# Four value-table buffers in the first stage, and another order of work at the opening of the second attention

## The reference

```python
def gat(x, adj, weight, linear_i, linear_j):           # layer 0, 8 heads of 64
    wh = (x @ weight).reshape(n, 8, 64)
    awh_i = (wh * linear_i).sum(axis=2); awh_j = (wh * linear_j).sum(axis=2)
    e = leaky_relu(awh_i[:, None, :] + awh_j[None, :, :], 0.2)
    e = e + ((1.0 - adj) * -1e10)[:, :, None]
    a = softmax(e, axis=1)
    return einsum('ijh,jhf->ihf', a, wh).reshape(n, 512)

def attention(x, adj, Wks, Wqs, Wvs, Wo):              # layer 1, 8 heads of 64
    adj = maximum(adj, eye)
    q, k, v = (einsum('nd,hdk->hnk', x, W) for W in (Wqs, Wks, Wvs))
    scores = einsum('hqk,hmk->hqm', q, k) * 64 ** -0.5
    scores = scores + 0.01 * eye - 1e16 * (1.0 - adj)
    return einsum('hqm,hmk,hko->qo', softmax(scores, axis=-1), v, Wo)

x = layernorm(x + gat(x, adj, ...))
x = layernorm(x + attention(x, adj, ...))
```

## Time and profile before

| | us |
|---|---|
| median of 3 runs | 4261.97 (4261.85 to 4263.58) |
| the profiled execution's own time | 4264.08 |
| its span, first to last instruction | 4260.6 |
| TensorE clock granted over the span | 0.952 of full |

### The profile page before, as it was taken

How to read it: one execution, slowest core, us unless ns; L and a number is a source line. 1 busy time by engine, 2 the same in 40 slices (tenths; PEclk the granted TensorE clock), 3 DMA queues, 4 the chain that set the end, 5 groups by cost and what they waited for, 6 DMA issues and landing times. The chain is left out here.

```text
span 4260.6 us, 104547 instructions
## 1 busy us (share of the span) xinstructions
PE 3773.0 (89%) x42884; PEld 2512.9 (59%) x42884; DVE 3499.7 (82%) x6039; ACT 3344.7 (79%) x4233; POOL 439.5 (10%) x635
## 2 busy tenths in 40 slices
PE   7981399999999969919999999999999999999977
PEld 4540399999999924405555555555555555555533
DVE  6655699999999977638888888888888888888734
ACT  3433699999999822209999999999999999999932
POOL 1211100000000000020120201201112011120000
PEclk9995699999999979959999999999999999999989
DMA  9988855555554377662453534444445354353133
GB/s 347 392 287 210 242 175 170 184 188 189 189 188 164 121 206 238 209 174 71 116 138 90 142 95 119 133 101 131 107 108 138 93 142 109 95 143 93 45 111 138
DMA packets 364121, 674.35 MB, mean 158 GB/s; under 512 B 79584, under 2 KB 239408, under 8 KB 326784
## 3 DMA queue, kind: packets, MB, share of 16 engines
q1 hardware_dynamic: 296448, 574.83, 45.3%
q0 software_dynamic: 24064, 84.37, 6.5%
q10 hardware_dynamic: 43136, 8.53, 1.0%
HBM read 524.43 MB, written 143.20 MB: 157 GB/s over the span
## 5 line engine op out<-in xcount | busy, mean ns | idle before, releaser
L1230 DVE CUSTOM_DVE_ANT_0 m_junk<-m_rough,m_rows 128x1024 bf16<-128x1024 f32 x1024 | 1253.5, 1224 | 287.8 <-PE m_rough L1097 226.3
L1179 ACT ACTIVATE m_scores<-m_strip 128x1024 f32<-128x1024 fp8e4 x1024 | 1052.3, 1028 | 102.4 <-POOL m_strip L1028 37.9
L1193 ACT ACTIVATE m_whole<-m_scores 128x1024 int32<-128x1024 f32 x1024 | 1038.0, 1014 | 35.9 <-PE m_scores L1130 25.5
L630 PE MATMUL g_acc<-g_vals,g_pos 128*128 128x130 f16 x8192 | 956.4, 218 | 48.6 <-DVE g_neg L585 48.6
L547 ACT ACTIVATE g_step<-g_arow,k_steep 128x512 fp8e4<-128x512 f32 x1536 | 948.6, 707 | 40.2 <-DVE g_pos L578 37.2
L630 PE MATMUL g_acc<-g_vals,g_neg 128*128 128x130 f16 x8192 | 955.8, 221 | 0.0
L1111 PE MATMUL m_acc<-m_v,m_halves 128*128 128x129 f16 (+1 forms) x16384 | 897.1, 208 | 45.2 <-ACT m_got L1156 45.2
L1111 PEld LDWEIGHTS m_acc<-m_v,m_halves 128*128 128x128 f16 x16384 | 751.0, 98 | 279.8 <-issue 186.5
L630 PEld LDWEIGHTS g_acc<-g_vals,g_pos 128*128 128x128 fp8e4 x8192 | 801.9, 98 | 59.5 <-DVE g_neg L585 37.1
L1125 PE MATMUL m_scores<-m_qA,m_kA 128*128 128x512 f16 x2048 | 780.7, 381 | 5.7 <-ACT m_scores L1179 5.6
L630 PEld LDWEIGHTS g_acc<-g_vals,g_neg 128*128 128x128 fp8e4 x8192 | 784.9, 96 | 0.0
(11 more groups left out here) (161 smaller groups left out, 3005.2 us busy)
## 6 DMA issues: line engine op xcount, KB each, us to landing
g_vals<-scr_gat_v SPq DMA_DIRECT2D x128, 1040.0 KB, 5.1
m_v<-scr_v SPq DMA_DIRECT2D x64, 1032.0 KB, 7.9
a_stage<-in_adj SPq DMA_DIRECT2D x64, 1024.0 KB, 9.3
m_kA<-scr_k_hi SPq DMA_DIRECT2D x128, 512.0 KB, 6.2
scr_row_mask<-a_rowm SPq DMA_DIRECT2D x64, 512.0 KB, 7.6
m_kB<-scr_k_lo SPq DMA_DIRECT2D x64, 512.0 KB, 5.4
m_rows<-scr_row_mask POOLq DMA_DIRECT2D x64, 512.0 KB, 7.3
scr_gat_v<-a_early POOLq DMA_DIRECT2D x32, 520.0 KB, 6.9
```

Source lines behind the costliest of these rows:

```text
L630: mm = pe.matmul(acc[:, b, it, lo:hi], edges[:, n % RING, t, rows], vals[:, b, 4 * j + t, lo:hi], start=j == 0 and t == 0 and lo == 0, sto ...
L1179: nc.scalar.activation(scores[:, n % 2], strip[:, 2 * st:2 * st + 2, :].rearrange("p t i -> p (t i)"), ACT.Copy, bias=-BIG, scale=BIG / ED ...
L1193: nc.scalar.activation(whole[:, st % 2], scores[:, st % 2], ACT.Exp, scale=0.125).then_inc(exped, 1)
L1230: nc.vector.tensor_tensor_reduce(out=junk[:, n % 2], in0=rough[:].rearrange("p a m -> p (a m)"), in1=rows[:, n % TC, n // TC * WIDE:(n // ...
```

## The change

- `tab` has four buffers (`TABS`), each with its own semaphore; ACT waits at tile t for the store of tile t - 4. `prod` keeps its four quarter buffers.
- At the opening of `attend`, POOL no longer writes the ones; it issues the 8 pieces of `rows` first, then the 8 of `strip`, then both fixes. DVE writes the ones ahead of its first max tile, and PE waits for them behind the 28 max tiles.
- SP issues the keys of unit 1 once 4 max tiles are taken, the rest of unit 0 once 8 are, and all the others once 16 are.
- The 28 early max tiles go in turn through three PSUM buffers: `rough` and the two of `scores`. PE waits with tile m until tile m - 3 has been taken. From tile 28 on the order is as before.
- The four matmuls that opened the banks are gone. ACT stores and loads the offset first and then seeds the two buffers of `scores`, when the last early tile that lies in each has been taken.

```diff
-        tab = early[:, 0:H * 2 * VG].bitcast(F16).rearrange("p (b h z v) -> p b h z v", b=2, h=H, z=2)
+        TABS = 4
+        tab = early[:, 0:TABS * H * VG].bitcast(F16).rearrange("p (b h z v) -> p b h z v", b=TABS, h=H, z=2)
...
-                b = t % 2
-                if t >= 2:
-                    act.wait_ge(tab_out[b], 16 * (t // 2))
+                b = t % TABS
+                if t >= TABS:
+                    act.wait_ge(tab_out[b], 16 * (t // TABS))
...
             load_keys(0)
+            sp.wait_ge(max_taken, TC)
             load_keys(1)
+            sp.wait_ge(max_taken, 2 * TC)
             load_rest(0)
+            sp.wait_ge(max_taken, TILES)
             load_keys(2)
             load_rest(1)
             load_keys(3)
...
-            nc.gpsimd.memset(kB[F:F + 1, :, :], 1.0).then_inc(ones_in, 1)
-            pool.wait_ge(ones_in, 1)
             for g in range(PIECES):
                 rows_piece(0, g)
+            for g in range(PIECES):
                 strip_piece(0, g)
             fix_rows(0)
             fix_strip(0)
...
+        def rough_of(m):
+            if m < EARLY and m % 3:
+                return scores[:, m % 3 - 1, :]
+            return rough[:].rearrange("p a m -> p (a m)")
...
-                if m >= 1:
+                if m >= EARLY:
                     pe.wait_ge(max_taken, m)
+                elif m >= 3:
+                    pe.wait_ge(max_taken, m - 2)
...
-            pe.wait_ge(keys_in[0], 64)
-            pe.wait_ge(ones_in, 1)
-            for bank in range(4):
-                mm = pe.matmul(scores[:, bank // 2, bank % 2 * CW:(bank % 2 + 1) * CW], kA[:, 0, 0:P], kA[:, 0, 0:CW], start=True, stop=True)
-            mm.then_inc(opened, 1)
             for m in range(EARLY):
                 max_tile(m)
+            pe.wait_ge(ones_in, 1)
...
-            act.wait_ge(opened, 1)
-            seed(0)
-            seed(1)
             store_offset(0)
             load_offset(0)
+            act.wait_ge(max_taken, EARLY - 2)
+            seed(0)
+            act.wait_ge(max_taken, EARLY - 1)
+            seed(1)
             unit(0, True)
...
                 tile_there(u, n)
+                if 2 <= m < EARLY:
+                    dve.wait_ge(max_taken, m - 1)
...
+            nc.vector.memset(kB[F:F + 1, :, :], 1.0).then_inc(ones_in, 1)
             for m in range(TILES):
                 take_max(m)
```

More of the change, by code:

```diff
@@ L174, in front @@
         exped, ready, mult, high, low = (s.sem(n) for n in ("exped", "ready", "mult", "high", "low"))
-        tab_out = [s.sem("tab_out0"), s.sem("tab_out1")]
+        tab_out = [s.sem(f"tab_out{b}") for b in range(TABS)]
         adj_in = [s.sem(f"adj_in{b}") for b in range(STAGES)]
@@ L241, in _ @@
                 pool.dma_start(scr.gat_v[:, :, t, :].rearrange("h p v -> p h v"),
-                               tab[:, t % 2].rearrange("p h z v -> p h (z v)")).then_inc(tab_out[t % 2], 16)
+                               tab[:, t % TABS].rearrange("p h z v -> p h (z v)")).then_inc(tab_out[t % TABS], 16)
             for b in range(2):
                 pool.wait_ge(a_out[b], 16 * C // 2)
-                pool.wait_ge(tab_out[b], 16 * NT // 2)
+            for b in range(TABS):
+                pool.wait_ge(tab_out[b], 16 * NT // TABS)
         @block.tensor
@@ L405, in _ @@
                     dve.wait_ge(high, 2 * t + z + 1)
-                    nc.vector.tensor_tensor(tab[:, b, :, z, F + 1:2 * F + 1], prod[:, 2 * b + z, :].rearrange("p (h f) -> p h f", f=F),
-                                            tab[:, b, :, z, 0:F], ALU.subtract).then_inc(low, 1)
+                    nc.vector.tensor_tensor(tab[:, t % TABS, :, z, F + 1:2 * F + 1], prod[:, 2 * b + z, :].rearrange("p (h f) -> p h f", f=F),
+                                            tab[:, t % TABS, :, z, 0:F], ALU.subtract).then_inc(low, 1)
             assert g == G
@@ L451, in _ @@
                     act.wait_ge(mult, 2 * t + z + 1)
-                    nc.scalar.copy(tab[:, b, :, z, 0:F], prod[:, 2 * b + z, :].rearrange("p (h f) -> p h f", f=F)).then_inc(high, 1)
+                    nc.scalar.copy(tab[:, b, :, z, 0:F], prod[:, 2 * (t % 2) + z, :].rearrange("p (h f) -> p h f", f=F)).then_inc(high, 1)
                 if t % 8 in (2, 5, 7):
@@ L950, in attend @@
         offset_ready, offset_out, offset_in = s.sem("offset_ready"), s.sem("offset_out"), s.sem("offset_in")
-        opened, seeded = s.sem("opened"), s.sem("seeded")
+        seeded = s.sem("seeded")
         inverted, strip_cleared = s.sem("inverted"), s.sem("strip_cleared")
@@ L1090, in max_tile @@
                     pe.wait_ge(keys_in[b], 64 * (u // KSLOTS + 1))
-                if m >= 1:
+                if m >= EARLY:
                     pe.wait_ge(max_taken, m)
+                elif m >= 3:
+                    pe.wait_ge(max_taken, m - 2)
+                to = rough_of(m)
                 for half in range(2):
@@ L1096, in max_tile @@
                     rows_at = slice(half * F, (half + 1) * F)
-                    mm = pe.matmul(rough[:, half, :], qC[rows_at, b, :].rearrange("k (p t) -> k p t", t=TC)[:, :, n % TC],
+                    mm = pe.matmul(to[:, half * CW:(half + 1) * CW], qC[rows_at, b, :].rearrange("k (p t) -> k p t", t=TC)[:, :, n % TC],
                                    kA[rows_at, b, at:at + CW], start=True, stop=True)
@@ L1228, in take_max @@
                 tile_there(u, n)
+                if 2 <= m < EARLY:
+                    dve.wait_ge(max_taken, m - 1)
                 gate(dve, passed_v)
-                nc.vector.tensor_tensor_reduce(out=junk[:, n % 2], in0=rough[:].rearrange("p a m -> p (a m)"),
+                nc.vector.tensor_tensor_reduce(out=junk[:, n % 2], in0=rough_of(m),
                                                in1=rows[:, n % TC, n // TC * WIDE:(n // TC + 1) * WIDE],
```

## The result

| | before | after |
|---|---|---|
| median, us (same chip, 4 runs each) | 4261.91 | 4195.38 (4191.47 to 4198.97) |
| ratio after/before, 95% interval | | 0.9843 (0.9830 to 0.9857) |
| profiled execution, us (span) | 4264.08 (4260.6) | 4191.47 (4189.7) |

The change takes 66.5 us off, where 75 were forecast. A later run of the same kernel gave a ratio of 0.9851 (0.9838 to 0.9865).

The account below looks back on a forecast made before the run. It saw two holes, the table stage (waits for table stores) and the opening of `attend`; gains 29 + 46 = 75 us off the profiled 4264.08 give 4189, 4187 at the median. Range 4172 to 4203, with B and C mostly in 4164 to 4210.

Parts of the forecast that it names:

- The two holes: Only the table stage (312 to 486 us) and the 97.5 us opening of `attend` could shrink; steady `attend` costed at nothing.
- Table stage, 145 us, gain 29: Table stage: with four table buffers, mostly DMA-limited at 257 GB/s, 174 us falls to 145; gain bounds 0 and 54.
- Compute floor, 120: Table stage: DVE's tiles and masks need 114 us, plus 6 us waiting for ACT after 8 flip copies.
- Tile 0 at 13.9 us into the block: Opening of `attend`: first max tile starts at 1834.2 us, after POOL's 12.05 us of issues and 1.63 us fix.
- Period 1.20: Opening of `attend`: early max tiles 1.20 us apart, set by DVE alone, instead of 2.10; bounds 1.15 and 1.31.
- A stall of 2.5 us at tile 12, behind rows: Opening of `attend`: SP's held-back loads slow the last `rows` pieces to 86 GB/s, so tile 12 waits 2.5 us.
- The offset has 12 us to spare: Opening of `attend`: offset asked for at 1856.4 us, its two trips have 12 us; before, 3.1 us to the second's issue.
- Opening 51.6 us, gain 46: Opening of `attend`: first exponential at 1871.9 us instead of 1917.81; gain 46 us, bounds 36 and 48.5.
- Rival A: Opening of `attend`: POOL held until DVE's memset ends, first exponential 7.9 us later, time 4195; 7%.
- B: Table stage stays bound by SP's bursts, 159 us, gain 15 or less, at the centre 12; time 4204; 15%.
- C: Table stage: DMA can exceed 257 GB/s, so compute decides, 120 + 4 us, gain 50; time 4166; 12%.
- D: Steady `attend`: 1024 steps fall into another order; 0.073 us a step eats the gain, 0.1 gives 4289; 3%.

Follow-up runs that it names:

- the run with the offset first: Changed kernel, but SP waits for unit 0's offset to land, not for 16 max tiles, before later units' loads: 4203.76 us, ratio 0.9847, opening 50.1.
- the rearranged opening: Changed kernel with unit 0's offset landing before later loads, unit 1's keys after 2 tiles, fix after 4 row pieces, ones by POOL last: 4209.37 us, ratio 0.9850.

## Why the prediction was right, point by point

- **The two holes, and nothing else.** Right: no other part moved by more than 2.6 us. The slices were misread, though: the PE row of before stands at 1 and 3 in slices 4 and 5, not at 0. The sum doesn't use it.
- **Table stage, 145 us, gain 29.** 146.5 and 27.5 in the profile beside the forecast. That the number fits so well is luck: seven other profiles have 158.5 to 159.7 us. The step "nearly all of the stage is then limited by DMA and not by buffers" was wrong in the form in which it was put. It looked at the table's buffers only. Bandwidth sets a floor of about 140 (139.0 and 143.6 us with four edge buffers); the changed kernel comes near it only where its edge stores land early enough, and in the later profiles it stops at 159, a gain of some 18. The profile of before showed the sign: edge stores took 11.0 us to land against 3.2 for row masks, with two buffers and groups two or three tiles apart.
- **Compute floor, 120.** 115.2 measured, with half of the tables' bytes gone. That is 1 us above the 114 of tiles and masks: the 0.8 us after each flip copy were mostly not there.
- **Tile 0 at 13.9 us into the block.** 14.3; the 12.05 and 1.63 us of POOL held, and DVE's memset took 10.30 of the 10.3 forecast. POOL's path set it, as forecast, but with less room: unit 0's keys landed only after 12.5 us, where I had 8.7. The split of the queues, 86 to 171 GB/s, was measured when POOL had just begun; with both loaded from the start it was nearer to even.
- **Period 1.20.** 1.15: DVE needs no gap at all between two tiles; the 1.20 carried a change of instruction.
- **A stall of 2.5 us at tile 12, behind rows.** There was none; a stall of 2.5 us came at tile 16, behind unit 1's keys. Same size, other transfer: the rows got more and SP's queue less than I gave them.
- **The offset has 12 us to spare.** Wrong, the one step of the opening that failed. I took 3.1 us for its first trip from a moment when the DMA engines were idle (2.5 us to landing there), and put no number on the second. In the same microseconds the change sends 5.8 MB of loads: 10.3 and 7.6 us. It cost 3 to 3.5 us, which the run with the offset first gives back.
- **Opening 51.6 us, gain 46.** 53.4 and 44.1, the offset less the faster tiles.
- **Rival A, POOL locked by DVE's memset.** Didn't happen: five of the eight row issues and all eight strip issues began while it ran, and the two groups took 5.93 and 5.97 us, 0.75 each as before. By the rule of the Trainium skill's page "SBUF — State Buffer", section "SBUF: two separate sides", they would have ended after it, if this memset used the two-port mode; the trace doesn't say whether it does. The other way round a hold does show in the rearranged opening: DVE stood there until POOL's memset ended.
- **B and C.** B, that bursts keep the stage long, priced it at 159 us, and that is what the later profiles show, with the edge stores as its mechanism and not table stores. C, compute as the bound, fails: with the waits for edge stores gone too the stage takes 139 to 144 us at a DMA share of 0.99 to 1.01, not 124. Its premise is right elsewhere: the DMA engines moved 348 GB/s from 1806 to 1812 us in after. **D**, a slower rhythm: 2153.5 against 2154.9 us.
- **The time.** Forecast 4187, measured 4195. Of the 8.4 us between them 2.4 are in the profiled execution, 4191.5 against 4189: 1.5 and 1.9 us less from the two holes, 1.9 more to drain the stores at the barrier, and small differences elsewhere that give 3 back. The other 6 are the way to the median: I had it 2.1 us below the profiled execution, and it lies 3.9 above.

## What to carry to other kernels

When buffers take away a wait, list every ring that shares the same queues: the next one to fill sets the time, and its stores' time to landing stands in the profile already. In this stage two rings had to be deepened together; the table buffers alone took 18 us off it, the edge buffers alone nothing, both 34. Price a small transfer by the traffic that will run beside it in the changed kernel, and have the bulk wait for it: three microseconds on idle engines were ten under load. And look at what runs on GpSimd beside a short VectorE instruction on the path: in one run a memset turned 0.17 us into 6.59.

## What the runs showed of the hardware

- The stage that is full of transfers differed between two profiles of one kernel far more than the one bound by an engine: the table stage took 146.5 and 159.2 us, the steady part of `attend` 2153.5 and 2155.0. Chip and execution weren't separated.
- A DVE memset of 10.30 us didn't hold up the DMA issues on POOL (13 of them began beside it and kept their 0.75 us). In the one run where the two met, a POOL memset of 10.33 us held up a DVE `tensor_scalar` of 128x4, SBUF to SBUF, until it ended, 6.59 us instead of 0.17; the max tiles that started beside the memset ahead of it kept their 1.22 us.
- The DMA rate of the table stage was 240 to 257 GB/s at shares of 0.93 to 1.01, in a mix of table stores in rows of 520 bytes with row masks, edges and adjacency loads. In the same block ahead of it, without the table stores, the whole of 107 to 275 us ran at 391 in the kernel before. That the short rows make the difference is likely but wasn't tried alone:

```profile
107.00:275.00 168.00, 157.27 (x1007) 95.42 (x1005) 109.42 (x120) 76.30 (x111) 29.16 (x21) 1.00 1.07 391
```
